# A 12-sublayer decoder on one core: weights loaded one sublayer ahead, set-up work moved, and a filter spectrum split anew between VectorE and ScalarE

## The reference, cut to what matters

```
x = x + L0_attn(layernorm(x))            # 8 heads
x = x + L0_xattn(layernorm(x), ctx)      # 8 heads of 128 over 1601 places
...
x = x + L1_xattn(layernorm(x), ctx)      # 16 heads of 8, scores clipped at 10000, softmax over 1601
x = x + L1_ffn(layernorm(x))             # 16 experts, each place to its best one, up to a capacity
...
x = x + L2_xattn(layernorm(x), ctx, masks)
x = x + L2_ffn(layernorm(x))             # attention, then 8 experts weighted by a softmax
x = x + L3_attn(layernorm(x))            # half of the places are picked by score, then 8 experts, best 2
...
x = x + L3_ffn(layernorm(x))             # attention, then 8 experts, best 2
```

```
dt = exp(log_dt);  dtA = dt[:, None] * (A_re + 1j * A_im)
dC = C * (exp(dtA) - 1) / A
K  = 2 * real(einsum('dn,dnl->dl', dC, exp(dtA[:, :, None] * arange(L))))
y  = irfft(rfft(x, 2 * L) * rfft(K, 2 * L).T)[:, :L] + x * D_skip
```

## Time and profile before

| | |
|---|---|
| time, median of 3 runs | 4991.45 us (4990.57 to 4994.34) |
| the profiled execution | 4982.04 us, its span 4980.3 us |
| busy share TensorE, VectorE, ScalarE, GpSimd | 73%, 62%, 37%, 6% |
| mean granted TensorE clock | 0.851 of full speed |
| DMA | 56.20 MB, mean 11 GB/s |

### The profile page before, as it was taken

One profiled execution on the slowest core, in us unless ns is written; L12 is line 12 of the kernel. 1 busy time (PEld: TensorE's weight loads), 2 busy tenths in 40 slices (PEclk: granted clock), 3 DMA queues, 4 the chain that ended last, 5 costly groups with the idle time before them and its releaser, 6 DMA issues. The chain is left out here.

```text
span 4980.3 us, 55000 instructions
## 1 busy us (share of the span) xinstructions
PE 3656.6 (73%) x21916; PEld 1974.3 (40%) x21922; DVE 3104.5 (62%) x4299; ACT 1859.8 (37%) x2001; POOL 308.3 (6%) x140
## 2 busy tenths in 40 slices
PE   4699999999999925677756760666543785679569
PEld 2434444444444313334335540422221453455346
DVE  4366666666666665698965448599984445442442
ACT  1255555555555412244431321244430343332123
POOL 1000000000000001000000001144420000000000
PEclk8799999999999957799987985666666887788799
DMA  2000000000000001000010001000002001000100
GB/s 70 2 0 0 0 1 0 0 0 1 0 1 0 7 6 25 10 13 8 1 49 33 2 1 49 1 0 0 0 0 62 16 1 40 1 1 1 42 2 5
DMA packets 12881, 56.20 MB, mean 11 GB/s; under 512 B 2082, under 2 KB 2594, under 8 KB 11971
## 3 DMA queue, kind: packets, MB, share of 16 engines
q1 hardware_dynamic: 12626, 52.70, 3.5%
HBM read 48.89 MB, written 0.52 MB: 10 GB/s over the span
## 5 line engine op out<-in xcount | busy, mean ns | idle before, releaser
L934 PE MATMUL banks<-L0x_q_context,L0x_context 96*128 96x512 f32 (+1 forms) x1632 | 741.9, 596 | 10.0 <-ACT L0x_ring L1028 9.3
L959 PE MATMUL banks<-L0x_ring,L0x_context_rows 128*97 128x512 f32 (+1 forms) x1632 | 737.5, 594 | 1.1 <-ACT L0x_ring L1014 1.1
L1028 ACT COPY L0x_ring<-banks 128x1024 f32<-128x1024 f32 (+1 forms) x416 | 413.0, 995 | 658.4 <-PE banks L934 658.4
L1078 DVE TENSOR_TENSOR L0x_maxima<-L0x_maxima,L0x_ring 128x1024 f32<-128x1024 f32 (+1 forms) x288 | 342.6, 1194 | 257.1 <-ACT L0x_ring L1028 256.0
L1059 DVE TENSOR_TENSOR L0x_ring<-L0x_ring,L0x_spread 128x2048 f32<-128x2048 f32 (+1 forms) x208 | 457.3, 2200 | 18.4 <-ACT L0x_spread L1002 18.4
L934 PEld LDWEIGHTS banks<-L0x_q_context,L0x_context 96*128 96x128 f32 (+1 forms) x1632 | 300.1, 188 | 396.7 <-issue 378.0
L959 PEld LDWEIGHTS banks<-L0x_ring,L0x_context_rows 128*97 128x97 f32 (+1 forms) x1632 | 262.0, 164 | 416.8 <-issue 413.4
L1014 ACT ACTIVATE L0x_ring<-L0x_ring 128x2048 f32<-128x2048 f32 (+1 forms) x208 | 384.1, 1847 | 11.4 <-DVE L0x_ring L1059 11.4
L1434 ACT ACTIVATE L1x_probs<-banks 128x2048 f32<-128x2048 f32 (+1 forms) x112 | 196.6, 1756 | 265.3 <-PE banks L1365 223.2
L1467 DVE TENSOR_REDUCE L1x_maxima<-banks 128x3 f32<-128x1203 f32 (+1 forms) x176 | 241.6, 1373 | 69.2 <-PE banks L1334 69.2
L1334 PE MATMUL banks<-L1x_k,L1x_q 32*128 32x401 f32 x1024 | 178.4, 582 | 116.7 <-DVE L1x_maxima L1467 102.5
(11 more groups left out here) (912 smaller groups left out, 5713.4 us busy)
## 6 DMA issues: line engine op xcount, KB each, us to landing
L1f_expert_weights<-in_L1f_experts SPq DMA_DIRECT2D x16, 512.0 KB, 9.4
L2f_expert_weights<-in_L2f_experts SPq DMA_DIRECT2D x8, 512.0 KB, 6.6
L3a_expert_weights<-in_L3a_experts SPq DMA_DIRECT2D x8, 512.0 KB, 6.4
L3f_expert_weights<-in_L3f_experts SPq DMA_DIRECT2D x8, 512.0 KB, 6.7
L1x_k<-L1x_k_rows SPq DMA_DIRECT2D x64, 50.0 KB
L0x_context_rows<-in_context_rows SPq DMA_DIRECT2D x1, 2448.0 KB, 27.9
L0x_context<-in_context SPq DMA_DIRECT2D x1, 2401.5 KB, 19.2
L1x_context<-in_context SPq DMA_DIRECT2D x4, 600.4 KB, 5.9
```

Of the source, the lines that this page charges most:

```text
L934: mm = pe.matmul(k.ps[0:height(j), i, :], c1[:, j * P:j * P + height(j)], q1[:, u // 2 % 2, :], start=True, stop=True)
L959: mm = pe.matmul(k.ps[0:CW, bank, :], rows1[0:height(j), j, :], ring[0:height(j), s % RING, i, :], start=s == FIRST[u] and i == 0, stop=s ...
L1028: act.copy(ring[0:r, s % RING, 2 * p:2 * p + len(pair), :], k.ps[0:r, 2 * p:2 * p + len(pair), :]).then_inc(copied, 1)
L1078: dve.tensor_tensor(o, before, ring[0:r, s % RING, 2 * p:2 * p + m, :], ALU.max).then_inc(maxed, 1)
```

## The change

1. `begin` does in one stage what four did. SP issues x, the first weights, the heads' weights, the context twice and L0_xattn's output bias; POOL makes the constants and two tables more (`count`, 1 up along columns, `number`, 1 up along partitions); VectorE writes the column of ones, one column of 97 instead of POOL's whole buffer.
2. `WeightsAhead` replaces `load_weights`: three buffers, and a sublayer's first stage issues the next one's loads. L0_ffn's are issued while L0_xattn's weights are folded.
3. Experts: two are issued in the stage of the gates, the rest in the stage that uses them.
4. `number` and `order` compute on VectorE, inside `linear_rows`, what POOL's stages made in L1_ffn and L3_attn.
5. `attend_clipped`: values 16 wide instead of 32, one more matmul at the start that writes the bank of sums, the scan a tick earlier, prepare, turn and add at other ticks and at other places in a tick.
6. L2_xattn and L2_ffn share buffers (tiles that were their own are now views of others).
7. `filter_spectrum`: ScalarE makes the mask row (Identity), the angles (16 multiplications of 128 x 128 each, twice) and the exponentials (16 each, twice). One reduced angle serves both sine and cosine: cos is Sin(pi/2 - |angle|). The first exponential is multiplied into U once, not into t1 and t2. Small sines and em1 come ahead of the large turn.

The diff, cut (the calls of `load_weights` become `k.weights.use(...)`; the turn is `sine` without its Sin and its wait):

```diff
-def make_constants(k):
+def begin(k, first):
 
     with k.stage() as (block, signal):
-        made = signal()
+        made, loaded = signal(), signal()
+        marks = 12
+
+        @block.sync
+        def _(sp):
+            sp.dma_start(k.x[:], k.dram["x"]).then_inc(loaded, 16)
+            if first:
+                k.weights.load(sp, first)
+            if k.context_ahead:
+                k.context_ahead.load(k, sp)
...
+            step.start(pool.iota(k.count[:], [[1, P]], base=1, channel_multiplier=0, allow_small_or_imprecise_dtypes=True))
+            step.start(pool.iota(k.number[:], [[1, 1]], base=1, channel_multiplier=1, allow_small_or_imprecise_dtypes=True))
+
         @block.vector
         def _(dve):
+            if k.context_ahead:
+                dve.memset(k.context_ahead.rows1[:, :, CD:], 1.0)
+            dve.wait_ge(made, marks)
             dve.tensor_reduce(k.row31[:], k.ident[:, 31::32], X, ALU.add)
 
...
-def load_weights(k, layer, ctx):
...
+HOME = {"L0_attn": 0, "L0_ffn": 0, "L1_attn": 1, "L1_xattn": 0, "L1_ffn": 1, "L2_attn": 0, "L2_xattn": 2, "L2_ffn": 0,
+        "L3_attn": 1, "L3_ffn": 0}
...
+    def use(self, layer):
+
+        (total, length), ahead = self.extent(layer), self.next(layer)
+        with self.k.stage() as (block, signal):
+            @block.sync
+            def _(sp):
+                if layer not in self.begun:
+                    self.load(sp, layer)
+                if ahead and HOME[ahead] != HOME[layer]:
+                    self.load(sp, ahead)
+                sp.wait_ge(self.here[layer], 16 * (bool(total) + bool(length)))
+        w = self.buffers[HOME[layer]]
...
+                k.weights.load(sp, "L0_ffn")
...
-                pool.memset(self.rows1[:], 1.0)
...
+    def load(self, k, sp):
+        sp.dma_start(self.heads[:], k.dram["L0x_heads"]).then_inc(self.here, 16)
+        sp.dma_start(self.c1[:].rearrange("c (b n) -> c b n", b=B), k.dram["context"].rearrange("b c n -> c b n")).then_inc(self.here, 16)
+        sp.dma_start(self.rows1[:, :, 0:CD], k.dram["context_rows"]).then_inc(self.here, 16)
+        sp.dma_start(self.bout[:], k.dram["L0_xattn_rows"].broadcast_to([P, P])).then_inc(self.here, 16)
...
+VW = 16
...
-SCAN_FROM, PREPARE_AT, TURN_AT, FLOOR_AT = -4, 7, 8, 9
+SCAN_FROM, GATHER_AT, PREPARE_AT, ADD_AT, FLOOR_AT = -5, 6, 7, 8, 9
...
-                        mm = pe.matmul(k.ps[row(h), 7, 0:S], v[0:height(j), b % 2, j, 4 * g + h, :],
+                        mm = pe.matmul(k.ps[32 * h:32 * h + VW, 7, 0:S], v[0:height(j), b % 2, j, 4 * g + h, :],
...
+            pe.matmul(k.ps[:, 7, 0:S], low[:, 1, 0, :], low[:, 1].rearrange("p t n -> p (t n)"), start=True, stop=True)
...
-                if i == TURN_AT and u + 1 < U:
+                if i == PREPARE_AT and u + 1 < U:
                     turn(u + 1)
                 for slot in slots_in(n):
...
+                if i == ADD_AT and u + 1 < U:
+                    add(u + 1)
                 clip(n)
                 for m in bursts_in(n):
                     reduce_(m)
-                if i == PREPARE_AT and u + 1 < U:
+                if i == GATHER_AT and u + 1 < U:
                     prepare(u + 1)
-                if i == TURN_AT and u + 1 < U:
-                    add(u + 1)
                 if i == PREPARE_AT and u % 4 == 2 and u // 4 + 1 < B:
...
+    EARLY = 2
...
+    def load(self, sp, some):
+        for e in some:
+            sp.dma_start(self.w[:, e].rearrange("p a f d -> p (a f d)"), self.dram[e]).then_inc(self.here[e], 16)
...
+                a.load(sp, range(a.EARLY, E))
...
+        def number(dve, step):
+            dve.memset(zeros[:], 0.0)
+            dve.tensor_copy(keepb[:], k.keep[:])
+            dve.tensor_scalar(places[:], k.count[:, 0:E], -1.0, E + 1.0, ALU.mult, ALU.add)
+            step(dve.tensor_scalar(starts[:], k.count[:, 0:E], -1.0, float(capacity), ALU.add, ALU.mult))
+            dve.tensor_scalar(own_slot[:], starts[:], k.number[:], None, ALU.add)
+            dve.tensor_tensor(numbers[:].rearrange("p (e n) -> p e n", e=E), k.count[:, None, 0:capacity].broadcast_to([P, E, capacity]),
+                              starts[:, :, None].broadcast_to([P, E, capacity]), ALU.add)
...
-                step = Steps(pool, made)
-                step(pool.memset(before[:], 1.0))
-                for it in range(TPB):
-                    step(pool.affine_select(out=before[:, it, :], in_=before[:, it, :], compare_op=ALU.is_gt, fill=0.0,
-                                            base=it * P, pattern=[[-1, S]], channel_multiplier=1))
...
+        def order(dve, step):
+            dve.tensor_scalar(places[:], k.count[:, 0:E], -1.0, E + 1.0, ALU.mult, ALU.add)
+            dve.tensor_tensor(strict[:], k.keep[:], k.ident[:], ALU.subtract)
+            for it in range(TPB):
+                for jt in range(TPB):
+                    o = before[:, it, jt * P:(jt + 1) * P]
+                    if jt == it:
+                        dve.tensor_scalar(o, k.keep[:], -1.0, 1.0, ALU.mult, ALU.add)
+                    else:
+                        dve.memset(o, float(jt < it))
+        linear_rows(k, [(hrT, w["w2"])], copy_product(s, w["b2"]), 1, order)
...
-                pool.iota(steps16[:, 0, :], [[1, LOW]], base=0, channel_multiplier=0, allow_small_or_imprecise_dtypes=True).then_inc(powers, 1)
-                pool.iota(steps16[:, 1, :], [[LOW, HIGH]], base=0, channel_multiplier=0, allow_small_or_imprecise_dtypes=True).then_inc(powers, 1)
-                pool.wait_ge(masks, 16)
-
-                pool.tensor_scalar(hidden[:], seen[:], 1.0, -MASKED, ALU.subtract, ALU.mult)
...
+                def multiply(out, rate, some):
+                    for n in range(LOW):
+                        mm = act.mul(out[:, :, n], rate, float(some * n))
+                    return mm
+
...
+                multiply(angle, th, 1).then_inc(multiples, 1)
+                act.wait_ge(rates, 3)
                 act.activation(x2, a, ACT.Exp).then_inc(exped, 1)
-                for n, t in enumerate((t1[:], t2[:], s2, x1)):
-                    act.wait_ge(sines, n + 1)
-                    act.activation(t, t, ACT.Sin).then_inc(sined, 1)
-                act.wait_ge(exps, 2)
-                act.activation(ev[:], ev[:], ACT.Exp).then_inc(exped, 1)
-                act.wait_ge(sines, 5)
+                for n in range(LOW):
+                    mm = act.activation(ev[:, :, n], a, ACT.Exp, scale=float(n))
+                mm.then_inc(exped, 1)
+                act.wait_ge(masks, 16)
+                act.activation(hidden[:], seen[:], ACT.Identity, scale=-MASKED, bias=quarter[0:1, 1:2])
+                act.wait_ge(bent, 1)
+                act.activation(s2, s2, ACT.Sin).then_inc(sined, 1)
+                act.wait_ge(bent, 2)
+                act.activation(x1, x1, ACT.Sin).then_inc(sined, 1)
+                act.wait_ge(bent, 3)
+                act.activation(t1[:], t2[:], ACT.Abs).then_inc(absolute, 1)
+                act.wait_ge(absolute, 1)
+                act.activation(t1[:], t1[:], ACT.Sin, scale=-1.0, bias=quarter[:, 0:1]).then_inc(sined, 1)
+                act.activation(t2[:], t2[:], ACT.Sin).then_inc(sined, 1)
+                act.wait_ge(kept, 1)
+                multiply(angle, th, LOW).then_inc(multiples, 1)
+                act.wait_ge(kept, 2)
+                for n in range(HIGH):
+                    mm = act.activation(ev[:, :, n], a, ACT.Exp, scale=float(LOW * n))
+                mm.then_inc(exped, 1)
+                act.wait_ge(bent, 4)
                 act.activation(V[:], V[:], ACT.Sin).then_inc(sined, 1)
 
             @block.vector
...
-                dve.tensor_tensor(ev[:], across(a), along(0), ALU.mult).then_inc(exps, 1)
-                step(dve.tensor_tensor(angle[:], across(th), along(0), ALU.mult))
-                sine(step, dve, (sines, sined, 1), angle[:], work[:], t1[:], 0.25, float(np.pi / 2))
-                sine(step, dve, (sines, sined, 2), angle[:], work[:], t2[:], 0.0, 0.0)
...
+                turn_angle(step, dve, nr, mag, s2, 0.0, 0.0).then_inc(bent, 1)
+                turn_angle(step, dve, th, mag, x1, 0.0, 0.0).then_inc(bent, 1)
...
+                turn_angle(step, dve, angle[:], work[:], t2[:], 0.0, 0.0).then_inc(bent, 1)
...
+                dve.wait_ge(sined, 4)
+                dve.sem_inc(kept, 1)
                 step(dve.tensor_tensor(t1[:], t1[:], across(cA), ALU.mult))
                 step(dve.tensor_tensor(t2[:], t2[:], across(cB), ALU.mult))
                 step(dve.tensor_tensor(U[:], t1[:], t2[:], ALU.add))
-
-                dve.tensor_tensor(ev[:], across(a), along(1), ALU.mult).then_inc(exps, 1)
-                step(dve.tensor_tensor(angle[:], across(th), along(1), ALU.mult))
-                sine(step, dve, (sines, sined, 5), angle[:], work[:], V[:], w["turns"], w["radians"])
+                dve.wait_ge(exped, 2)
+                dve.tensor_tensor(U[:], U[:], ev[:], ALU.mult).then_inc(kept, 1)
+
```

247 lines of the change are left out of this document (113 added, 134 removed).

## The result

The changed kernel takes 4843.95 us (median of four runs, 4841.5 to 4856.31) where the kernel before takes 4991.01: ratio 0.971, 95% interval 0.9692 to 0.9727. The forecast was 4825, in a range of 4808 to 4846; the ratio times the 4991.45 us of the table before gives 4847, the upper end of that range. The direction was right and most of the terms too; the saving was 147 us where 166 were forecast. The profiled execution took 4841.5 (span 4839.8), 140.5 less than that of before.

A forecast was written before the change was run, and what follows sets the result against it. No engine bounds the kernel as a whole; idle stretches at stage barriers count in full. Terms 13.0 + 64.6 + 23.3 + 10.0 + 48.5 + 7.0 = 166.4 off 4982.04 give 4815.6, plus 9.4 is 4825 us; range 4808 to 4846.

The forecast's parts named there:

- Start: Kernel's start: all loads issued under POOL's constants, VectorE normalises at 12.0 instead of 27.95; 13.0 us saved, 11 to 16.
- Rival B: A wait returns: the start's fetch costs 8 us more, or an expert or weight lands late; 4833 to 4850, chance 0.12.
- L1_ffn: L1_ffn's start: POOL's iota stage and the reversed-places stage go, arithmetic moves into linear_rows; 23.3 us saved, 21 to 24.
- L3_attn: L3_attn: VectorE's idle 7.93 and 2.14 us at POOL's stages go, new work lies in linear_rows; 10.0 us saved.
- Weights and experts: SP's waits for weights, three expert stages and barriers go, loads hidden a layer ahead; 64.6 us saved, 62 to 67.
- Spectrum: Filter spectrum: 113.2 us become 64.6, VectorE stays the bound and ScalarE meets its due times; 48.5 saved, 41 to 49.
- rival A: ScalarE binds in the spectrum, strided writes at 0.6 us or more; 7.5 to 15 us more, 4833 to 4840, chance 0.12.
- L1_xattn: L1_xattn's loop: new order saves about 3 us in plain units, 6 with fills, head costs 2.3; total 7, -5 to 14.
- rival C: TensorE's clock is granted higher at layer beginnings with shorter idle stretches; 5 to 10 us less, 4815 to 4820, chance 0.06.
- The offset: Whole kernel: the median lies 9.4 us over the profiled run, added to 4815.6 to give 4825.
- The bounds of the terms: Whole kernel: term ranges taken as independent give about 10 us below and 15 above the forecast.

The follow-up runs named there:

- old ticks: The changed kernel with L1_xattn's ticks as in the kernel before, the 16 wide values and first matmul left in: 4855.09 us (0.9739).
- contexts late: The changed kernel with heads' weights and both context loads issued in the stage after POOL's constants, output bias ahead of them: 4828.85 us (0.9678).

## Why the prediction was right or wrong

**Start: the step that failed**, 17.1 of the 25.9 us by which the two profiled executions miss the sum. "All loads go out under POOL's constants" took an issue to cost what the rows of issues show, 0.4 to 0.7 us, whatever is on the queue. That held in the kernel before, where no load was issued behind the context rows. Behind them 64 KB of bias waited 27.19 us, which the barrier passed to VectorE; put ahead of them it took 0.44, and the start came to 16.18, near the 15 of the text. Rival B had a stall at this place of 8 us, by the other mechanism, POOL's fetch under traffic; that one was priced at 3.0 and was 4.9 (12.72 less 7.82).

**L1_ffn: a second failed step**, 5.7. The text took the POOL stage's 12.08 us for something that goes with the iotas (whose own work is 1.4, not a fraction of one); what stands ahead of them is a stall of POOL's next operation after a PARTITION_ALL_REDUCE (in the changed kernel at 2566.07, L1_xattn's flag), be it the iota or the subtraction. Removing the iotas passed it on, 8.1 us to the subtraction and 9.04 more of waiting to VectorE; 3 came back, since VectorE no longer ran beside POOL. In L3_attn the same kind of stall had no POOL operation left to go to: 10.0 forecast, 10.0 measured. There the prediction had its two waits the wrong way round, which leaves the sum as it is: the 7.93 are for the places, the 2.14 for the affine_selects, as POOL's row of before shows:

```profile
4200.27 0.14 POOL L1892 IOTA L3a_places<- 128x8 f32 x1 [82.52 <-issue]
```

Not every operation pays. This COPY, the first after L0_ffn's reduce (1745.07) but with memsets between them, starts in the changed kernel 0.2 us behind VectorE in its stage, and so do the memsets:

```profile
1963.45 2.85 POOL L1487 COPY L1x_k<-row_of_each_head 128x3202 f32<-128x3202 f32 x1 [20.42 <-POOLq L77]
```

Ahead of each stalled operation, and not ahead of this COPY or a memset, the trace has a record of POOL's sequencer, MODIFY_POOL_CONFIG. The record alone is not the stall: in the kernel before one stands 0.1 us ahead of a product at 60.53. From it to the operation are 6.9 to 7.3 us with little or nothing on the queues (L3_attn before; L1_ffn's subtraction with the experts in stages of their own) and 10.5 beside sixteen experts' loads (L1_ffn before). The Trainium skill (GPSIMD Engine Reference, Instruction dispatch) has the first call to a freshly loaded kernel pay about 6 us of loading, with no visible instruction; the runs have 6.9 to 13.2 at the start, with nothing on POOL's row meanwhile, and show that it returns within one program and grows with the traffic. That these stalls are such a loading is the likely reading; no run shows what is moved.

**Weights and experts**: right, 65.6 against 64.6. No matmul of an expert waited for a load in the changed kernel, as the slack of 10 to 23 us said.

**Spectrum**: right, by its steps too: 64.4 against 64.6, and rival A is refuted, the strided operations took 0.23 us. The ScalarE chain ran ahead of its due times by more than forecast. The Trainium skill (ScalarE: Activation LUTs, What ACT_TABLE_LOAD costs) would have put the small sines 2.8 us later by its drains; in the trace the load takes 1.28 (2978.54), the operation before it ends as it starts and the sine starts 0.01 after it, so the measurement decides for the row. The Trainium skill's rule that identity, copy and abs are in every table set (ScalarE: Activation LUTs, Table sets: the hidden batching unit) holds: no load stands ahead of the Abs at 2985.12, nor of the Identity at 2972.95.

**L1_xattn**: 7.5 against 7.0, the total in part by luck. The head of the loop cost nothing (73.6 us to the first addition against 73.4), where 2.8 were forecast; the intervals with the fills gave 4.8 where 6 were forecast, the plain ones at the end 2.3 where all plain ones were to give 3.

**The unedited part**: 6.8 lost in L3_xattn to the granted clock, which rival C had as a gain with "5 to 10 less". Its sign was wrong.

**The offset**: the forecast added 9.4 us from the profiled run to the median; for the changed kernel that distance is 2.4. These 7.0 went the other way, so that 25.9 in the sum became 19 in the time. That is luck: in the experiments the profiled run lies from 7.4 us under its median (old ticks) to 3.3 over it (contexts late). The bounds of the terms, taken as independent, also give 8 below the forecast, not 10.

## What to carry to other kernels

Price an issue by what stands in its queue, not by its own row: 64 KB behind the context rows held SP, and the barrier behind it, until these had nearly landed, so small loads go first. When an idle time in front of an operation shows no releaser, ask which operation comes next if that one is removed: a stall that isn't the operation's own moves to it, as it did from the iotas to the subtraction. A change of serial work is worth its sum almost exactly (four of the six terms came within 1.0 us); what misses are the side effects on queues and on the clock.

## What was not expected of the hardware

- An issue on SP of 64 KB took 27.19 us behind 2.4 MB of context rows (pieces of 384 bytes, 544 packets of 4608 in the trace), and 0.44 ahead of them; sixteen issues of 512 KB in a row took at most 1.05 each in the kernel before.
- POOL's silent stall at the start: 6.9 to 7.8 us on idle queues, 9.7 to 9.9 with 1.6 MB on them, 12.0 to 13.2 with 8.6 MB; after a PARTITION_ALL_REDUCE it returns ahead of the first iota or subtraction (8.1 and 9.5 in L1_ffn), not ahead of a memset or of L1_xattn's COPY.
- ScalarE writes 128x128 at a stride of sixteen elements in 0.23 us each when sixteen follow one another; two contiguous sines in a row (2979.83 and 2980.05) start 0.22 apart, so the stride costs next to nothing.
- A POOL tensor_scalar of 21.84 us holds a VectorE product for 21.11, even one of 128x128; 21 of the spectrum's 49 us go when POOL gets the row back.
- A TensorE stream unchanged in its instructions took 4.5 us more in 77 at a lower granted clock (0.90, not 0.96); the stretch around it is alike, 492.8 to 494.1 us, in nine kernels that have the changed weights and experts.
